# Four bilinear corners weighted and summed in one VectorE instruction each, two biases moved to ScalarE, and a sum of two branches moved to TensorE

## The chip, the cores and the metric

The kernel runs on one core of a Trainium2 chip. The metric is the device time of one execution in microseconds. A core has TensorE (PE, matrix products into PSUM), ScalarE (ACT), VectorE (DVE), GpSimd (POOL, which here issues the indirect gathers) and SyncE (SP, which issues the other transfers). Each engine works through its own list of instructions in order, and the lists meet only in semaphores.

## The reference, cut to what matters

Per image (32 images, 96 channels, 48 x 48 pixels) a first layer ends in `out = (out_mamba + silu(batchnorm(lc))) * gate`, then a 96 x 96 projection, a residual, a layer norm and an MLP whose roundings to half precision and to 8 bits are part of the reference. A second layer is a deformable 3 x 3 convolution: each of the nine taps of a pixel reads the normalised image at a fractional place.

```python
def _bilinear(img, py, px):
    ...
    return (1 - wy_) * (1 - wx_) * v00 + (1 - wy_) * wx_ * v01 + wy_ * (1 - wx_) * v10 + wy_ * wx_ * v11
...
def _qlinear(x, W, b):
    y = q_acc(jnp.einsum('bsk,nk->bsn', q_mul(x), q_mul(W)))
    return q_acc(y + q_mul(b))
```

The samples, times a mask, go through a 9 x 96 x 96 product, again with a residual, a layer norm and an MLP of 384 hidden channels.

## The kernel before

Pass one computes the scan branch and the local branch of all images and stores both. Pass two, which the diff touches, reads them back and does everything else. It walks through **periods** `w` of one chunk of 384 pixels (eight rows): an image has six periods, and a period has twelve **places** `u`. In one period four chunks of work at different stages run side by side: chunk `c` (projection, norm 1, MLP 1), chunk `d` (norm 2's result into the padded image and into a table of corner rows), chunk `e` (deformable convolution, norm 3, MLP 2) and chunk `f` (the last step of MLP 2). Three tiles of 128 pixels are sampled per period, four places for each tile. The order on each engine is written out by hand: every engine's block runs over the same list of `(w, u)` and issues what belongs to a place.

**Sampling.** GpSimd gathers for each tap of a tile one row of 4 corners x 96 channels into `G` (ring of four tiles, nine indirect transfers a tile, issued two tiles ahead). VectorE then treats a tile in two halves (taps 0 to 3, taps 4 to 8). `multiply` (places 0 and 2 of the tile) copies the weights of the half to PSUM, multiplies corner 0 into a PSUM accumulator (L1910) and the corners 1 to 3 in place (L1912). `add_corner` (places 1 and 3) adds them in three instructions (L1925 twice, L1927). TensorE transposes the sums (L1641), ScalarE copies them to `cols_t` (L1791), and at place 3 of a later period `convolve` (L1654) multiplies nine taps into bank BN.

**MLP.** `hidden` (L1678, TensorE) gives three blocks of 128 hidden channels, `rounded` (L1812, ScalarE) rounds them to half precision, `biased` (L1948, VectorE, places 7 and 11) adds the bias and clips at zero, `quantized` (L1819, ScalarE) rounds to 8 bits, `second` (L1686, TensorE) multiplies back. ScalarE rounds the result into `y16` (L1869 or L1832), and `residual` (VectorE, places 9 and 1) adds the second bias (L1955) and the residual (L1957).

**Projection.** At place 0 VectorE writes `xflat` (L1975, the scaled result of norm 2) and adds the local branch to `mix` (L1980). At place 1 TensorE projects `mix` with the gated weights (L1711) and transposes `xflat` (L1721). At place 2 VectorE adds that to `x_t` (L1992) and ScalarE copies the transposed rows to `prow` (L1842). `convolve` waits for `prow`, since bank BN is shared. Behind it TensorE centres `x_t` (L1661), ScalarE squares, TensorE averages (L1668), ScalarE forms the inverse deviation in two steps (L1802, L1805), and VectorE writes `xq` at place 5 (L1940). The chunk `e` does the same with `x3` (L1935, place 5) and ends in another L1940 at place 8. In the last period of an image ScalarE applies SiLU to the whole local branch of the next one (L1881) between two table loads. In two periods of six VectorE computes `positions` (L1550 to L1569) at place 1: those of 12 tiles in one, of 6 in the other.

## Time and profile before

| | us |
|---|---|
| median of three timed runs | 17210.08 |
| lowest and highest | 17208.7, 17227.91 |
| span of the profiled execution (first to last instruction) | 17175.7 |
| median run less that span | 34.4 |
| pass one in that span | 10393 |
| pass two in that span | 6783 |

The profiled execution's own time is shown only as its span; what lies around the span is taken as the 34.4 us by which the median run exceeds it. In the rows below, a timeline row gives the start, the busy time, engine, line, output<-input, the shapes and how many instructions are merged; in square brackets the idle time of the engine before it and what ended the wait. "Places" of the text can be read off by the line numbers.

### The profile page before, as it was taken

The page shows a single profiled execution, that of the slowest core. Times are in us where ns is not written, and L with a number is a line of the kernel's source. Part 1 is how long each engine was busy: PE and PEld are TensorE (multiplying, and loading weights), DVE is VectorE, ACT ScalarE, POOL GpSimd, SP SyncE. Part 2 cuts the span into 40 slices and gives each one's busy share as a digit, 9 for nine tenths or more (in the row PEclk, how much of TensorE's full clock was granted, in tenths as well). Part 3 has the DMA queues.
Part 4 walks back from the last instruction along what each step waited for, and adds up shares of the span by engine and source line. Part 5 has one row for each costly group of instructions (what it writes and reads, how often), then busy time and mean ns, then how long its engine had stood idle before and what let it go on. Part 6 is the DMA issues. An engine that isn't in the chain of part 4 may idle for free. (4 is left out here: it accounts for less than half of the span.)

```text
span 17175.7 us, 183440 instructions
## 1 busy us (share of the span) xinstructions
PE 12732.8 (74%) x51055; PEld 6059.9 (35%) x51055; DVE 14514.2 (85%) x19220; ACT 8968.6 (52%) x16380; POOL 12401.2 (72%) x10756
## 2 busy tenths in 40 slices
PE   6777777777777777777787646777777777777776
PEld 3333333333333333333333312333333333333333
DVE  5888888888888888888888855988898989899998
ACT  4555655656556555565565534444444444444443
POOL 3777777777777777777777744777777777777776
PEclk9999998999999998999999867888888888888887
DMA  2333333333433333333433335666666666666665
GB/s 55 94 97 96 99 100 98 99 95 96 104 94 95 101 98 98 98 98 99 101 97 95 96 90 137 186 187 186 186 188 185 186 192 188 188 188 186 187 188 155
DMA packets 1297936, 2234.90 MB, mean 130 GB/s; under 512 B 713341, under 2 KB 759125, under 8 KB 1284629
## 3 DMA queue, kind: packets, MB, share of 16 engines
q1 hardware_dynamic: 896022, 1090.20, 25.1%
q0 software_dynamic: 368640, 1076.24, 22.3%
q10 hardware_dynamic: 32256, 56.64, 1.1%
q8 instruction: 425, 6.96, 0.2%
q14 instruction: 593, 4.86, 0.1%
HBM read 1493.27 MB, written 275.76 MB: 103 GB/s over the span
## 5 line engine op out<-in xcount | busy, mean ns | idle before, releaser
L1623 POOL DMA_INDIRECT G<-corners,idx x5184 | 4964.2, 958 | 1992.1 <-issue 1554.4
L1383 POOL TENSOR_TENSOR hc<-h,crep 128x768 f32<-128x768 f32 x2304 | 4176.4, 1815 | 2206.5 <-DVE h L1157 1233.9
L1141 DVE TENSOR_TENSOR ps<-dxr,ps 128x768 f32<-128x768 f32 x2304 | 2186.3, 949 | 1041.2 <-PE ps L750 1024.9
L1157 DVE TENSOR_TENSOR_SCAN h<-decay,carry,ps 128x768 f32<-128x768 f32 x1536 | 2776.4, 1808 | 145.5 <-ACT decay L972 85.3
L761 PE MATMUL ps<-hc,sel 128*96 128x512 f32 (+1 forms) x6144 | 2581.8, 548 | 353.4 <-POOL hc L1383 198.7
L972 ACT ACTIVATE decay<-dtr,a_neg 128x768 f32<-128x768 f32 x2304 | 2117.8, 926 | 348.2 <-DVE h L1157 332.8
L750 PE MATMUL ps<-bq,pick 128*128 128x512 bf16 (+1 forms) x4608 | 1233.8, 353 | 991.3 <-DVE h L1157 806.1
L1912 DVE TENSOR_TENSOR G<-G,ps 128x1152 f32<-128x1152 f32 (+1 forms) x1152 | 1724.7, 1497 | 0.0
L761 PEld LDWEIGHTS ps<-hc,sel 128*96 128x96 f32 x6144 | 1022.7, 182 | 1608.1 <-issue 1204.8
L1654 PE MATMUL ps<-cols_t,w_def 128*96 128x384 f32 x3456 | 1342.5, 550 | 178.3 <-ACT prow L1842 172.2
L869 PE MATMUL ps<-xcp,w_local 128*96 128x384 f32 x3456 | 1436.8, 538 | 40.7 <-POOL xcp L1357 39.2
L1925 DVE TENSOR_TENSOR ps<-ps,G 128x384 f32<-128x384 f32 (+1 forms) x2304 | 1407.4, 611 | 47.1
L1157 DVE TENSOR_TENSOR_SCAN h<-decay,ps 128x768 f32<-128x768 f32 x768 | 1342.2, 1748 | 32.3 <-ACT decay L972 2.5
L980 ACT ACTIVATE carry<-h 128x1 f32<-128x1 f32 x1536 | 303.0, 197 | 1934.4 <-DVE h L1157 1932.8
L810 PE MATMUL ps<-xnp,w_conv 128*96 128x384 f32 x3456 | 1292.6, 513 | 24.5 <-ACT x_in L1009 22.3
L1797 ACT ACTIVATE sq<-ps 96x384 f32<-96x384 f32 x576 | 280.1, 486 | 1944.1 <-PE ps L1661 1944.1
L1641 PE MATMUL ps<-ident,G 128*128 128x128 f32 x5184 | 1005.9, 311 | 94.2 <-DVE G L1927 93.1
L750 PEld LDWEIGHTS ps<-bq,pick 128*128 128x128 bf16 x4608 | 377.7, 101 | 1803.2 <-DVE h L1157 923.5
L1791 ACT ACTIVATE cols_t<-ps 128x512 f32<-128x512 f32 (+1 forms) x1728 | 832.8, 483 | 324.2 <-PE ps L1641 323.1
L1641 PEld LDWEIGHTS ps<-ident,G 128*128 128x128 f32 x5184 | 764.0, 162 | 466.6 <-issue 282.9
L1654 PEld LDWEIGHTS ps<-cols_t,w_def 128*96 128x96 f32 x3456 | 626.5, 187 | 831.3 <-issue 598.1
L1686 PE MATMUL ps<-hq,w2q 128*96 128x384 fp8e5 x1152 | 312.0, 389 | 773.8 <-ACT rs L1805 489.4
(243 smaller groups left out, 23803.3 us busy)
## 6 DMA issues: line engine op xcount, KB each, us to landing
crep<-c_rows SPq DMA_DIRECT2D x3072, 96.0 KB
dtr<-rel SPq DMA_DIRECT2D x2304, 96.0 KB, 2.2
dxr<-one_e SPq DMA_DIRECT2D x2304, 96.0 KB
corners<-prow SPq DMA_DIRECT2D x1536, 72.0 KB
G<-corners,idx POOLq DMA_INDIRECT x5184
x_in<-in_x SPq DMA_DIRECT2D x32, 864.0 KB, 6.6
local_all<-local_c ACTq DMA_DIRECT2D x192, 144.0 KB
sim<-sorted_rows SPq DMA_DIRECT2D x32, 864.0 KB, 6.8
```

The source lines that it names most:

```text
L750: m = pe.matmul(wide(bank_of("step", s), P)[:, a:b], Wt["pick"][:, ng, :], M["tall"]["bq"][:, q % 2, a:b], start=True, stop=True)
L761: m = pe.matmul(wide(BY, C)[:, a:b], Wt["sel"][:, cg, :], hc[:, v % HC, a:b], start=(v % ROUND == 0), stop=(v % ROUND == ROUND - 1))
L869: m = pe.matmul(ps[0:C, BV, 0:CH], Wt["w_local"][:, t, :], M["tall"]["xcp"][:, 8 * c + t // 3:8 * c + t // 3 + 8, t % 3:t % 3 + W], start= ...
L972: act.activation(decay[:, s % 3, :], dtr[:, q % 2, cg, :], ACT.Exp, scale=Wt["a_neg"][:, direction(q)[0], ng, cg:cg + 1]).then_inc(S["s_de ...
L1141: dve.tensor_tensor(drive, dxr[:, q % 2, cg, :], drive, ALU.mult).then_inc(S["s_drive"], 1)
L1157: dve.tensor_tensor_scan(along(h[:, v % HR, :], k), along(decay[:, v % 3, :], k), along(wide(bank_of("step", v % STEPS), P), k), first, AL ...
L1383: pool.tensor_tensor(hc[:, v % HC, :], h[:, v % HR, :], crep[:, g % CRING, :], ALU.mult).then_inc(S["s_weighted"], 1)
L1623: pool.indirect_dma_start(M["G"][:, slot(g), k, :], None, table(r), bass.IndirectOffsetOnAxis(M["idx"][side(r)][:, t, k:k + 1], 0)).then_i ...
L1641: m = pe.transpose(ps[:, BT + n % 2, (k % 4) * P:(k % 4 + 1) * P], M["G"][:, slot(t - 1), k, 0:P], ident[:])
L1654: m = pe.matmul(ps[0:C, BN, 0:CH], Wt["w_def"][:, k, :], M["cols"][:, of_e(w)[1] % 2, k, :], start=(k == 0), stop=(k == TAPS - 1))
L1912: dve.tensor_tensor(rows[:, :, 1:], rows[:, :, 1:], by[:, :, 1:].unsqueeze(3).to_broadcast([P, n, CORNERS - 1, C]), ALU.mult).then_inc(S[" ...
L1925: dve.tensor_tensor(acc[:, 0:n], acc[:, 0:n], rows[:, :, q], ALU.add).then_inc(S["p_half"], 1)
```

## The change

VectorE's `multiply` becomes one product over all four corners of the half, in place. `add_corners` sums them with one `tensor_reduce` over the corner axis, that is, it reads four words 96 words apart for each word it writes. The sums of the first half go to a new buffer `samp`, those of the second half over the first half's rows in `G`. The weights are copied to PSUM once in six tiles. ScalarE takes both biases: `biased` in three instructions (one at place 6 or 10, two at 7 or 11), and a second instruction in `returned`. The local branch is no longer added on VectorE: TensorE projects `mix` and `local_t` one after the other into the same bank.

```diff
-                dve.tensor_copy(ps[:, BW, wat:wat + CORNERS * n],
-                                M["wts"][side(r)][:, t, k0:k1].rearrange("p k q -> p (k q)")).then_inc(S["p_wset"], 1)
-                dve.wait_ge(S["p_wset"], at + 1)
-                dve.tensor_tensor(acc[:, 0:n], rows[:, :, 0], by[:, :, 0:1].to_broadcast([P, n, C]),
-                                  ALU.mult).then_inc(S["p_half"], 1)
-                dve.tensor_tensor(rows[:, :, 1:], rows[:, :, 1:],
-                                  by[:, :, 1:].unsqueeze(3).to_broadcast([P, n, CORNERS - 1, C]),
+                if half == 0:
+                    dve.wait_ge(S["p_wset"], n // WGROUP + 1)
+                k0, k1, rows = corners(g, half)
+                by = weights_of(g)[:, k0:k1]
+                dve.tensor_tensor(rows, rows, by.unsqueeze(3).to_broadcast([P, k1 - k0, CORNERS, C]),
                                   ALU.mult).then_inc(S["p_mul"], 1)
...
-                if q < CORNERS - 1:
-                    dve.tensor_tensor(acc[:, 0:n], acc[:, 0:n], rows[:, :, q], ALU.add).then_inc(S["p_half"], 1)
-                else:
-                    dve.tensor_tensor(rows[:, :, 0], acc[:, 0:n], rows[:, :, q], ALU.add).then_inc(S["p_prod"], 1)
+            def add_corners(g, half):
+
+                n = nth(of_tile, g)
+                dve.wait_ge(S["p_mul"], 2 * n + half + 1)
+                if half == 0 and n >= 2:
+                    dve.wait_ge(S["p_tturn"], 3 * (n - 2) + 1)
+                if half == 1:
+                    dve.wait_ge(S["p_prod"], 2 * n + 1)
+                k0, k1, rows = corners(g, half)
+                dve.tensor_reduce(sampled(g, k0, k1), rows.rearrange("p k q c -> p k c q"), AX.X,
+                                  ALU.add).then_inc(S["p_prod"], 1)
...
+            def set_weights(g):
+
+                r, t = of_tile(g)
+                n, size = nth(of_tile, g), CORNERS * TAPS * WGROUP
+                if n >= WGROUP:
+                    dve.wait_ge(S["p_mul"], 2 * (n - WGROUP))
+                at = size * (n // WGROUP % 2)
+                dve.tensor_copy(ps[:, BW, at:at + size],
+                                M["wts"][side(r)][:, t:t + WGROUP].rearrange("p t k q -> p (t k q)")
+                                ).then_inc(S["p_wset"], 1)
...
+            def biased(kind, w, b1, first, last):
+
+                i = turn[kind, w]
+                if first == 0 and turn_before(kind, w):
+                    act.wait_ge(S["p_quant"], NHID * turn_before(kind, w))
+                for j in range(first, last):
+                    act.wait_ge(S["p_rnd"], NHID * i + j + 1)
+                    act.activation(r16[:, KIND[kind], j, :], h16[:, KIND[kind], j, :], ACT.Relu,
+                                   bias=b1[:, j:j + 1]).then_inc(S["p_bias"], 1)
+
+            def returned(n, place, z, b2, done):
+
+                act.wait_ge(S["p_lin" + n], place + 1)
+                act.activation(y16[:, z, :], ps[0:C, BV, 0:CH], ACT.Copy).then_inc(S["p_yr" + n], 1)
+                act.wait_ge(S["p_yr" + n], place + 1)
+                if place:
+                    act.wait_ge(S[done], place)
+                act.activation(z16[:, z, :], y16[:, z, :], ACT.Identity, bias=b2).then_inc(S["p_yb" + n], 1)
...
                 if u == 7 and c is not None:
+                    biased("c", w, Wt["b1q"][0], 1, NHID)
                     quantized("c", w)
...
-                    pe.wait_ge(S["p_mix"], nc_ + 1)
                     if w % NCH == LASTP:
+                        pe.wait_ge(S["p_mamba"], 16 * (next_before(w) + 1))
+                        pe.wait_ge(S["p_silu"], next_before(w) + 1)
                         pe.wait_ge(S["p_gate"], next_before(w) + 1)
...
-                    pe.matmul(ps[0:C, BM, 0:CH], M["tall"]["wg"][:], M["tall"]["mix"][:, part(c[1])], start=True,
-                              stop=True).then_inc(S["p_proj"], 1)
+                    for name in ("mix", "local_t"):
+                        m = pe.matmul(ps[0:C, BM, 0:CH], M["tall"]["wg"][:], M["tall"][name][:, part(c[1])],
+                                      start=(name == "mix"), stop=(name == "local_t"))
+                    m.then_inc(S["p_proj"], 1)
```

The load of the next local branch now waits for the projection instead of the sum.

## Rows read from the trace of the kernel before

**Rows 1.** The page: span and busy time of each engine.

```profile
span 17175.7 us, 183440 instructions
PE 12732.8 (74%) x51055; PEld 6059.9 (35%) x51055; DVE 14514.2 (85%) x19220; ACT 8968.6 (52%) x16380; POOL 12401.2 (72%) x10756
```

**Rows 2.** Windows: pass two, then three periods; stretch: length, PE, PEld, DVE, ACT, POOL, PEclk.

```profile
10393.00:17175.70 6782.70, 4939.76 (x18916) 2443.76 (x18915) 6001.51 (x11201) 3192.66 (x7145) 4964.19 (x5184) 0.80 0.66 184
...
13143.71:13184.79 41.08, 26.69 (x100) 12.38 (x101) 35.21 (x71) 20.75 (x41) 26.58 (x28) 0.79 0.55 150
13184.79:13217.26 32.47, 24.25 (x100) 12.49 (x101) 29.67 (x53) 16.00 (x38) 24.54 (x27) 0.82 0.65 180
13217.26:13253.02 35.76, 25.96 (x100) 12.95 (x101) 33.64 (x71) 15.80 (x38) 27.09 (x29) 0.83 0.63 176
```

**Rows 3.** Timeline of VectorE over one ordinary period.

```profile
13075.42 0.55 DVE L1975 TENSOR_TENSOR xflat<-ps,rs 96x384 f32<-96x384 f32 x1 [0.57 <-ACT rs L1805]
...
13090.71 0.55 DVE L1940 TENSOR_TENSOR xq<-ps,rs 96x384 fp8e5<-96x384 f32 x1 [2.73 <-ACT rs L1805]
...
13098.59 0.55 DVE L1940 TENSOR_TENSOR xq<-ps,rs 96x384 fp8e5<-96x384 f32 x1
13099.06 0.16 DVE L1907 COPY ps<-wts 128x16 f32<-128x16 f32 x1
...
13101.15 0.32 DVE L1955 TENSOR_SCALAR z<-y,b2q 96x384 f16<-96x384 f16 x1
...
13109.56 0.55 DVE L1975 TENSOR_TENSOR xflat<-ps,rs 96x384 f32<-96x384 f32 x1 [0.56 <-ACT rs L1805]
```

**Rows 4.** Timeline of TensorE in the first half of that period.

```profile
13075.38 0.66 PE L1686 MATMUL ps<-hq,w2q 128*96 128x384 fp8e5 x3 [3.63 <-ACT rs L1805]
...
13076.52 1.57 PE L1711 MATMUL ps<-mix,wg 128*96 128x384 f32 x2
...
13079.88 7.52 PE L1654 MATMUL ps<-cols_t,w_def 128*96 128x384 f32 x18 [0.94 <-ACT prow L1842]
```

**Rows 5.** Timeline of ScalarE in its second half.

```profile
13098.03 0.52 ACT L1805 ACTIVATE rs<-rs 96x384 f32<-96x384 f32 x1
13098.46 1.33 ACT L1819 ACTIVATE hq<-r 128x384 fp8e5<-128x384 f16 x3
...
13100.63 0.49 ACT L1869 ACTIVATE y<-ps 96x384 f16<-96x384 f32 x1 [0.36 <-PE ps L1686]
...
13107.06 1.35 ACT L1819 ACTIVATE hq<-r 128x384 fp8e5<-128x384 f16 x3 [2.54 <-DVE r L1948]
```

**Rows 6.** VectorE's groups of the whole span, shapes kept apart: busy, mean ns.

```profile
L1912 DVE TENSOR_TENSOR G<-G,ps 128x1440 f32<-128x1440 f32 x576 | 948.7, 1647 | 0.0
L1912 DVE TENSOR_TENSOR G<-G,ps 128x1152 f32<-128x1152 f32 x576 | 776.0, 1347 | 0.0
...
L1925 DVE TENSOR_TENSOR ps<-ps,G 128x384 f32<-128x384 f32 x1152 | 645.3, 560 | 20.4
...
L1206 DVE TENSOR_REDUCE rlen<-unit 128x19 f32<-128x1824 f32 x32 | 65.2, 2038 | 2.0 <-ACT unit L1026 2.0
...
L1569 DVE TENSOR_TENSOR wts<-up,pos 128x108 f32<-128x108 f32 x64 | 22.8, 357 | 0.0
...
L1566 DVE TENSOR_TENSOR up<-wlow,sig 128x108 f32<-128x108 f32 x32 | 8.7, 272 | 1.1
```

**Rows 7.** Timeline of GpSimd: one of its gathers.

```profile
13102.03 0.95 POOL L1623 DMA_INDIRECT G<-corners,idx  x1 [0.30 <-issue]
```

**Rows 8.** Timeline of VectorE: change of image, then (last row) the small `positions` period.

```profile
13147.23 0.55 DVE L1980 TENSOR_TENSOR mix<-mix,local_t 96x384 f32<-96x384 f32 x1 [2.96 <-ACT local_t L1881]
...
13164.92 0.55 DVE L1940 TENSOR_TENSOR xq<-ps,rs 96x384 fp8e5<-96x384 f32 x1
...
13233.87 0.55 DVE L1940 TENSOR_TENSOR xq<-ps,rs 96x384 fp8e5<-96x384 f32 x1
```

**Rows 9.** Window of one microsecond behind TensorE's pause: PEclk is the granted clock.

```profile
13077.00:13078.00 1.00, 1.00 (x3) 0.33 (x2) 1.00 (x2) 0.77 (x2) 0.70 (x2) 0.50 0.65 191
```

More of the change, by code:

```diff
@@ L380, in build_program @@
                      "p_ctr3", "p_sq3", "p_var3", "p_rs3", "p_xq3", "p_lin3", "p_yr3", "p_yb3", "p_y", "p_out",
-                     "p_wset", "p_mul", "p_half", "p_prod", "p_tturn", "p_cols", "p_conv", "p_x3",
+                     "p_wset", "p_mul", "p_prod", "p_tturn", "p_cols", "p_conv", "p_x3",
                      "p_idx", *[f"p_got{i}" for i in range(GRING)])
@@ L1412 @@
 WTILES = 12
+WGROUP = 6
 def pass_two_memory(sbt, ctx):
@@ L1424, in pass_two_memory @@
     return dict(
-        tall=tall, x2=[low("x2_0", [L]), low("x2_1", [L])], x_t=low("x_t", [L]), local=b("local_t", [C, L]),
+        tall=tall, x2=[low("x2_0", [L]), low("x2_1", [L])], x_t=low("x_t", [L]), local=low("local_t", [L]),
         mix=low("mix", [L]), wg=low("wg", [C]), xn=low("xn2", [PH, PW]), xflat=b("xflat", [C, CH]),
@@ L1435, in pass_two_memory @@
         wts=[b(f"wts{i}", [P, NT, TAPS, CORNERS]) for i in range(2)],
-        G=b("G", [P, GRING, TAPS, CORNERS * C]), cols=b("cols_t", [P, 2, TAPS, CH]), x3=low("x3", [L]))
+        G=b("G", [P, GRING, TAPS, CORNERS * C]), samp=b("samp", [P, 2, SPLIT, P]), cols=b("cols_t", [P, 2, TAPS, CH]), x3=low("x3", [L]))
 def pass_two(nc, ps, S, M, Wt, dram, stages, has, image):
@@ L1522, in landed, with sampled @@
         return sum(slot(w) == slot(g) for w in issued if w <= g)
+    def sampled(g, k0, k1=None):
+        if k0 < SPLIT:
+            ap = M["samp"][:, nth(of_tile, g) % 2]
+        else:
+            k0, k1 = k0 - SPLIT, k1 and k1 - SPLIT
+            ap = M["G"][:, slot(g), 0:SPLIT].rearrange("p k c -> p (k c)")[:, 0:(TAPS - SPLIT) * P].rearrange(
+                "p (k c) -> p k c", c=P)
+        return ap[:, k0] if k1 is None else ap[:, k0:k1, 0:C]
     turns = []
@@ L1896, in multiply @@
             def multiply(g, half):
-                r, t = of_tile(g)
-                at = 2 * nth(of_tile, g) + half
+                n = nth(of_tile, g)
                 if half == 0 and g >= AHEAD:
                     dve.wait_ge(S[f"p_got{slot(g)}"], 16 * TAPS * landed(g))
-                k0, k1, rows, by = corners(g, half)
-                n = k1 - k0
-                if at:
-                    dve.wait_ge(S["p_mul"], at)
-                    dve.wait_ge(S["p_prod"], at)
-                dve.tensor_copy(ps[:, BW, wat:wat + CORNERS * n],
-                                M["wts"][side(r)][:, t, k0:k1].rearrange("p k q -> p (k q)")).then_inc(S["p_wset"], 1)
@@ L1940, in normalize, with residual @@
                 dve.tensor_tensor(dst[:], ps[0:C, bank, 0:CH], rs[:], ALU.mult, **cast).then_inc(S[done], 1)
-            def biased(kind, w, b1):
-                dve.wait_ge(S["p_rnd"], NHID * (turn[kind, w] + 1))
-                if turn_before(kind, w):
-                    dve.wait_ge(S["p_quant"], NHID * turn_before(kind, w))
-                for j in range(NHID):
-                    m = dve.tensor_scalar(r16[:, KIND[kind], j, :], h16[:, KIND[kind], j, :], b1[:, j:j + 1], 0.0,
-                                          ALU.add, ALU.max)
-                m.then_inc(S["p_bias"], 1)
-            def residual(n, c, place, z, b2, res, dst, bsem, done):
-                dve.wait_ge(S["p_yr" + n], place + 1)
-                dve.tensor_scalar(z16[:, z, :], y16[:, z, :], b2, None, ALU.add).then_inc(S[bsem], 1)
-                dve.wait_ge(S[bsem], place + 1)
+            def residual(n, c, place, z, res, dst, done):
+                dve.wait_ge(S["p_yb" + n], place + 1)
                 dve.tensor_tensor(dst[:, part(c)], res[:, part(c)], z16[:, z, :], ALU.add).then_inc(S[done], 1)
@@ L1975, in _ @@
                     dve.tensor_tensor(M["xflat"][:], ps[0:C, BM, 0:CH], M["rs"][:], ALU.mult).then_inc(S["p_xn"], 1)
-                if u == 0 and c is not None:
-                    if p == LASTP:
-                        dve.wait_ge(S["p_silu"], next_before(w) + 1)
-                        dve.wait_ge(S["p_mamba"], 16 * (next_before(w) + 1))
-                    dve.tensor_tensor(M["mix"][:, part(c[1])], M["mix"][:, part(c[1])], M["local"][:, part(c[1])],
-                                      ALU.add).then_inc(S["p_mix"], 1)
                 if p == 1 and u == 1 and has(k):
@@ L1986, in _ @@
                 if u == 1 and f is not None:
-                    residual("3", f[1], nf, 1, Wt["b2q"][1][:], M["x3"], M["x3"], "p_yb3", "p_y")
+                    residual("3", f[1], nf, 1, M["x3"], M["x3"], "p_y")
                 if u == 2 and c is not None:
@@ L1996, in _ @@
                     normalize("1", nc_, BM, M["rs"], M["xq"], "p_xq1", saturate=False)
-                if u == 7 and c is not None:
-                    biased("c", w, Wt["b1q"][0])
                 if u == 8 and e is not None:
@@ L2001, in _ @@
                 if u == 9 and c is not None:
-                    residual("1", c[1], nc_, 0, Wt["b2q"][0][:], M["x_t"], x2[side(c[0])], "p_yb1", "p_x2")
-                if u == 11 and e is not None:
-                    biased("e", w, Wt["b1q"][1])
+                    residual("1", c[1], nc_, 0, M["x_t"], x2[side(c[0])], "p_x2")
                 if of_tile(t) is not None and sub % 2 == 0:
+                    if sub == 0 and of_tile(t)[1] % WGROUP == 0:
+                        set_weights(t)
                     multiply(t, sub // 2)
                 if of_tile(t) is not None and sub % 2 == 1:
-                    for q in range(1, CORNERS):
-                        add_corner(t, sub // 2, q)
+                    add_corners(t, sub // 2)
                 if e is not None and u == 5:
```

40 lines of the change are left out of this document (17 added, 23 removed).

## The prediction, made before the changed kernel ran

> **What bounds the kernel now.** I read the page first for the engines' shares, then the windows by stage, then the timelines of one period. The page shows VectorE busiest with 85% of the span [rows 1]. Only pass two is touched: 6783 us, in which VectorE is busy for 6002, TensorE for 4940, ScalarE for 3193, GpSimd for 4964 [rows 2]. That share is an average. The length of a period varies: 32.5 us in an ordinary one, 35.8 with the small share of `positions`, 41.1 at the change of image [rows 2], and 34.1 for the ordinary period of the timelines [rows 3]; per image the one of each special kind stands beside four ordinary ones.
>
> The timeline shows two halves with different limits. First half, from `xflat` to `xq`: 15.29 us, and VectorE waits 2.73 us at its end [rows 3]. It is a chain through TensorE: `second`, four transposes, projection (started 1.14 us after `second`), transposes of `xflat`, `prow` on ScalarE, then the convolution, 7.52 us for 18 passes, then norm 1 [rows 4]. Second half, from `xq` to the next `xflat`: 18.85 us, in which VectorE waits only 0.56 us [rows 3]. It seems to be bound by VectorE, but two other engines arrive nearly with it: rs of norm 3 ends at 13098.55 [rows 5], and the second L1940 begins at 13098.59 [rows 3]; `y` ends at 13101.12 [rows 5] and `z` begins at 13101.15 [rows 3]. So work taken from VectorE is paid out only as far as these chains allow, and the change lengthens both.
>
> **The products.** 1152 words take 1347 ns and 1440 take 1647 [rows 6], 1.042 ns a word. Extended, 1536 words are 1.75 us and 1920 are 2.15. The product of corner 0, one of its kind a half, and the copy of the weights go. In a queue with no wait an instruction starts some 0.08 us before its forerunner ends: the COPY begins 0.47 us after an xq of 0.55 [rows 3].
>
> **The sums.** Three adds of 384 words (560 ns each [rows 6]) become one reduction that reads 1536 words; for the other half it is 480 and 1920. The trace has a reduction of 1824 adjacent words, 2038 ns [rows 6], so at that rate, with the slope above, 1.74 and 2.14 us: nothing is saved against three adds of 0.56 (1.68). It has none that reads with a hop. What it has is a product that writes every fourth word: 357 ns for 108 words against 272 for the same product written densely, so 0.79 ns more for each word that hops [rows 6]. Applied to the words read, the two reductions are 1.74 + 1536 x 0.79 ns = 2.96 us and 2.14 + 1920 x 0.79 ns = 3.66. The bounds are therefore 1.74 and 2.96, and 2.14 and 3.66. I take the upper ones: a tile's corners lie 96 words apart, no two successive reads adjoin, and the row that is nearest in the pattern is the hopping one, though it hops on the write side.
>
> The Trainium skill (Vector Engine (DVE) Microarchitecture Reference, section 5.2 on measured stream behaviour) says that a port streams at full rate only over runs of at least two adjacent 4-byte words, and gives about 1.73 ns a column for a two-source operation with one source hopping each element. By that figure, as an estimate, the reductions would be 2.8 and 3.5 us and the end some 90 us earlier than by the row. The same section lists a one-source operation alternating between two regions at the full rate, which is the rival below; no run here shows either yet.
>
> **Second half of the period.** VectorE, counted from `xq`, by starts: xq 0.47, first reduction 2.87, x3 at 3.34 (before 2.13), take 0.53, product 2.18, reduction 3.57: the L1940 of norm 3 can go at 9.62. Its own chain hangs on x3 and is 1.21 later than now: 7.88 + 1.20 = 9.08, so VectorE decides. Then 0.47, product 1.67, at 11.76. Here `z` is awaited. ScalarE now puts two bias instructions between rs and hq. Three hq take 1.33 us and one about 0.49, so the spacing is 0.42 to 0.43 [rows 5]: 0.86 for the two. And `z` runs on ScalarE behind `y`, 0.51 instead of VectorE's 0.32 [rows 3]. The residual add, now at 10.79, moves to 10.79 + 1.20 + 0.86 + 0.17 = 13.02, so VectorE waits 1.26 us. Then residual 0.47, reduction 2.87, product 2.18, reduction 3.66: `xflat` at 22.2 against 18.85, +3.4 us. ScalarE's own tail there (three more bias instructions 1.3 us, `z` 0.45, the first two 0.86: 2.6 in all) is paid nearly whole by its present wait of 2.54 us for VectorE's `r` [rows 5]; that chain ends at 18.9 + 1.2 = 20.1 and is hidden as long as the reductions are slow. If they aren't, it bounds the half at 18.9, no better than now.
>
> **First half.** The second projection pair costs what the first does: 1.57 us long, 1.36 from start to start, at a granted clock of 0.50 [rows 4, 9], that is, 1.2 GHz after the pause of 3.63 us [rows 4]. The removed add (0.47 on VectorE) doesn't help: TensorE is in its transposes until 13076.52 in any case. The slow stretch ends during the convolution now: its 18 passes average 0.42 us where the projection's two, with the same columns, average 0.79 [rows 4]. If it still ends at the same time, part of the 1.36 returns, since two passes of the convolution slide out of the slow stretch: 0.7 to 1.4, I take 1.0, so 16.3. VectorE's list, with waits for `z` and the projection met in time, is 0.47 + 1.67 + 0.47 + 2.87 + 0.53 + 2.18 + 3.57 + 1.78 = 13.5 us, hidden.
>
> **Special periods.** `positions` is the busy time by which VectorE exceeds that of an ordinary period: 33.64 - 29.67 = 4.0 us for the small share, 35.21 - 29.67 = 5.5 for the large one [rows 2]; I add 0.2 for the gaps between its short instructions. With the small share the first half takes 16.6 us now (13217.26 to 13233.87 [rows 2, 8]); it becomes 13.5 + 4.2 = 17.7: +1.1. At the change of image VectorE now stands 2.96 us at L1980 for SiLU [rows 8]; that wait moves to TensorE. The half takes 21.2 us now (13143.71 to 13164.92 [rows 2, 8]). Afterwards VectorE needs 13.5 + 5.7 = 19.2, and the chain is SiLU's end at 3.5 us (13147.23 less 13143.71), the projection pair and what follows it in an ordinary period (15.3 - 1.1), with the second pair's 1.4: 19.1. I take 19.3, -1.9. Its second half takes 19.9 now and 22.2 then: +2.3. Transfers: the local branch is requested with `mix`, one projection later, and is wanted a period later, so it is hidden. The wait of the reductions for `p_tturn` is for transposes two tiles back, so nothing queues there. `set_weights` is one short copy in six tiles, 96 in all.
>
> **Sum.** Per image 4 x (1.0 + 3.4) + (1.1 + 3.4) + (-1.9 + 2.3) = 22.5 us; 32 images 720 us. 17176 + 720 = 17896 of span, and with the 34 us around it 17930.
>
> **The rivals.**
> A, the reduction reads at the full rate. For it: 2038 ns for 1824 words, one word a cycle [rows 6]. Against it: those words adjoin. Then the second half is bound by ScalarE at 18.9 (+0.1) and the first by TensorE (+1.0): ordinary +1.1; small share 16.3 - 16.6 + 0.1 = -0.2; change of image -1.9 - 1.0 = -2.9. Sum 1.3 us an image, 42 us: 17250, and with 0.7 to 1.4 for the pair 17210 to 17300.
> B, faster: as A, but the second projection pair costs the chain nothing, because the slow clock ends sooner once TensorE is given that work. Then ordinary periods stay, and what VectorE gains where it binds is kept: 0.0 - 1.2 (small share) - 2.9 - 0.5 (tail of ScalarE shorter than reckoned, 0.1 each period) = -4.6 at best, -147 us, and half of it likelier: 17130. It decides from a full-rate reduction and a pair that adds under 0.3 us an ordinary period. A floor stands below: 27 gathers a period at 0.95 + 0.30 us each [rows 7] are 33.7 us, or 6480 of the 6783 over 192 periods.
> C, hopping costs a whole cycle or more and the longer pauses keep TensorE at the low clock through the convolution: 2.0 ns a word gives 18140, and a further microsecond a period 18300.
>
> **How the numbers follow.** Forecast (reads at 1.6 to 2.0 ns a word) 0.55, its own range 17780 to 18140; A 0.28; B 0.12; C beyond 18140 0.05. The range has to reach A and leaves B's deep end and C out: 17160 to 18140. A measurement tells about 0.2%, 34 us, from no change. Faster by that: B, 0.12, and a little of A, 0.02: 0.14. Within: the lower half of A, 0.14. Slower: the forecast, C and the rest of A, 0.72.
>
> **What would show it.** The two reductions' mean ns (2960 and 3660, or 1740 and 2140) decide first. VectorE's wait before the residual add at place 9, some 1.3 us, on ScalarE's `z`. L1711's successor as four matmuls of about 0.8 us or less in front of the transposes. VectorE's wait before `xq` near 2.8 us (5.5 under A). The wait at L1980 gone and one on TensorE for SiLU in its place. ScalarE's wait for `r` gone. The prediction is wrong if the reductions run at the dense rate, or if the pair is absorbed.

## The result and the profile after

The changed kernel takes 17792.63 us (median of 4 runs, 17774.59 to 17811.11) against 17209.39 for the kernel before: ratio 1.0334, 95% interval 1.0322 to 1.0347, so 583 us slower. The span grew by 597 us, from 17175.7 to 17772.6, all of it in pass two: counted from the first `xflat` (at 10341.5 us before, 10317.3 now) it grew by 621, while what lies ahead of it took 24 less, which is within what it differs by between the traces of these runs (10317 to 10373). The page (busy time of each engine), then the window over pass two:

```profile
span 17772.6 us, 179148 instructions
...
PE 13286.3 (75%) x51439; PEld 6323.8 (36%) x51439; DVE 15213.1 (86%) x12982; ACT 9751.4 (55%) x17916; POOL 12341.4 (69%) x10756
```

```profile
10393.00:17772.60 7379.60, 5485.87 (x19246) 2704.92 (x19246) 6711.85 (x4973) 3959.49 (x8648) 4904.74 (x5184) 0.75 0.60 169
```

VectorE issues 6200 instructions fewer in pass two and is busy 710 us longer (6711.85 less 6001.51 [rows 2]). The groups of the changed kernel between 12000 and 16000 us (count, busy us, mean ns, idle time before) say which:

```profile
L1963 DVE TENSOR_REDUCE G<-G 128x480 f32<-128x1920 f32 x315 | 1097.6, 3484 | 10.8
L1963 DVE TENSOR_REDUCE samp<-G 128x384 f32<-128x1536 f32 x315 | 879.0, 2790 | 0.0
L1951 DVE TENSOR_TENSOR G<-G,ps 128x1920 f32<-128x1920 f32 x315 | 674.2, 2140 | 0.0
...
L1951 DVE TENSOR_TENSOR G<-G,ps 128x1536 f32<-128x1536 f32 x315 | 549.0, 1743 | 5.8 <-DVE ps L1938 0.5
...
L1834 ACT ACTIVATE r<-h,b1q 128x384 f16<-128x384 f16 x630 | 361.1, 605 | 0.0
...
L1844 ACT ACTIVATE z<-y,b2q 96x384 f16<-96x384 f16 x210 | 129.1, 615 | 6.8
L1722 PE MATMUL ps<-local_t,wg 128*96 128x384 f32 x208 | 124.3, 690 | 0.0
...
L1982 DVE TENSOR_TENSOR x<-x_t,z 96x384 f32<-96x384 f32 x105 | 58.9, 561 | 195.7 <-ACT z L1844 195.7
```

The products cost the words at 1.04 ns, as before [rows 6]. The reductions take 2.79 and 3.48 us; the three additions they replace took 1.68 (3 x 0.56 [rows 6]) and 1.98 (3 x 0.66). The last line is VectorE waiting 195.7 us in 105 periods for `z`, now on ScalarE: 1.86 us each, 1.98 in the mean of the ordinary periods. The same period seen in time, on VectorE and then on ScalarE and TensorE:

```profile
13077.73 0.55 DVE L1977 TENSOR_TENSOR xq<-ps,rs 96x384 fp8e5<-96x384 f32 x1 [1.60 <-ACT rs L1817]
13078.20 2.80 DVE L1963 TENSOR_REDUCE samp<-G 128x384 f32<-128x1536 f32 x1
...
13087.06 0.53 DVE L1977 TENSOR_TENSOR xq<-ps,rs 96x384 fp8e5<-96x384 f32 x1
13087.53 1.73 DVE L1951 TENSOR_TENSOR G<-G,ps 128x1536 f32<-128x1536 f32 x1
13091.08 0.55 DVE L1982 TENSOR_TENSOR x<-x_t,z 96x384 f32<-96x384 f32 x1 [1.82 <-ACT z L1844]
...
13099.81 0.56 DVE L2000 TENSOR_TENSOR xflat<-ps,rs 96x384 f32<-96x384 f32 x1
```

```profile
13086.73 1.11 ACT L1834 ACTIVATE r<-h,b1q 128x384 f16<-128x384 f16 x2
13087.74 1.33 ACT L1850 ACTIVATE hq<-r 128x384 fp8e5<-128x384 f16 x3
...
13090.43 0.61 ACT L1844 ACTIVATE z<-y,b2q 96x384 f16<-96x384 f16 x1
```

```profile
13062.03 1.17 PE L1695 MATMUL ps<-hq,w2q 128*96 128x384 fp8e5 x3 [0.87 <-ACT rs L1817]
...
13063.85 1.49 PE L1722 MATMUL ps<-mix,wg 128*96 128x384 f32 x2
13065.13 1.49 PE L1722 MATMUL ps<-local_t,wg 128*96 128x384 f32 x2
...
13068.41 6.02 PE L1663 MATMUL ps<-cols_t,w_def 128*96 128x384 f32 x18 [0.94 <-ACT prow L1872]
```

From `xq` to `xflat` it is 22.08 us here (13077.73 to 13099.81), against 18.85 [rows 3]. In the first half the second projection starts 1.28 us behind the first. The convolution starts 5.90 us after `xflat` (which begins at 13062.51), where it was 4.46, and takes 6.02 us where it took 7.52 [rows 3, 4]: it ends 11.9 us after `xflat` in the one and 12.0 in the other. The granted clock shows why. Two windows of this period, then one of the period before the change [rows 3, 4]; the last number but two is the granted clock, 1.00 is 2.4 GHz and 0.50 is 1.2 GHz.

```profile
13066.00:13067.00 1.00, 1.00 (x5) 0.59 (x4) 1.00 (x1) 0.00 (x0) 0.00 (x0) 0.50 0.00 0
13068.00:13069.00 1.00, 0.59 (x2) 0.41 (x3) 1.00 (x3) 0.15 (x1) 0.69 (x2) 0.99 0.01 1
```

```profile
13082.00:13083.00 1.00, 1.00 (x3) 0.44 (x2) 1.00 (x2) 0.00 (x0) 0.70 (x2) 0.54 0.93 161
```

Now the clock is at its upper level 5.5 us after `xflat`, before the convolution. In the period before the change it came back 7.5 us after `xflat`, inside the convolution.

The period shown before the change was not the usual one. The ordinary periods of a trace are of two kinds: in some the whole convolution runs at the upper level and takes 6.02 us, in the others it starts at the lower one and takes 7.8. Before the change 85 of 123 are of the first kind, with a first half of 13.88 us, and 38 of the second, with 15.87, like the 15.29 of the rows. In the changed kernel 114 of 115 are of the first kind, with 14.62.

The periods of each run can be cut at `xflat` and at the two L1940 (`xq`, and the one for `e`). Means in us over 10450 to 17100 us, by kind of period, worked out from the VectorE timelines; "1st half" is from `xflat` to `xq`, the names are those of the experiments below:

```
                            ordinary (4 an image)       small positions     change of image
                          1st half  2nd half  total     1st   2nd  total    1st   2nd  total
before                      14.50     18.94   33.43   16.52 18.72  35.24  21.17 18.83  40.00
changed                     14.63     22.44   37.08   17.52 21.61  39.13  19.08 22.31  41.39
dense_reads                 15.14     20.11   35.25   15.23 20.17  35.39  19.61 19.00  38.61
two_adds                    17.10     20.08   37.18   15.80 19.43  35.23  19.50 19.43  38.93
two_adds_one_input          15.22     19.15   34.37   15.66 18.82  34.48  19.19 20.35  39.54
mix_on_vector               14.66     22.47   37.13   17.97 21.61  39.58  22.02 22.06  44.08
biases_on_vector            14.33     21.84   36.17   18.01 21.71  39.71  19.38 21.70  41.08
branches_on_tensor          14.91     18.85   33.76   16.27 18.98  35.25  19.04 19.10  38.14
branches_on_tensor_twice    14.96     19.01   33.97   16.44 18.71  35.16  18.40 18.85  37.25
biases_on_scalar            15.10     20.10   35.19   16.16 20.32  36.48  20.83 20.32  41.15
corners_only                15.18     21.86   37.03   18.35 21.69  40.05  22.14 21.68  43.83
```

Changed less before: 4 x 3.65 + 3.89 + 1.39 = 19.9 us an image, 636 us over 32 images, against the 621 from the first `xflat` on (probably because not every chunk is in work in the first and last periods).

### The profile page after: what moved, and what is told of

The parts are those of the page before. It is cut to its first block and busy times, and to the rows that moved or that the text cites. A ratio compares the mean times of both kernels' runs of the same rounds, so it can differ in the third digit from the quotient of the medians.

```text
span 17772.6 us, 179148 instructions
## 1 busy us (share of the span) xinstructions
PE 13286.3 (75%) x51439; PEld 6323.8 (36%) x51439; DVE 15213.1 (86%) x12982; ACT 9751.4 (55%) x17916; POOL 12341.4 (69%) x10756
## 5 line engine op out<-in xcount | busy, mean ns | idle before, releaser
L1633 POOL DMA_INDIRECT G<-corners,idx x5184 | 4904.7, 946 | 2668.5 <-issue 1419.6
L1951 DVE TENSOR_TENSOR G<-G,ps 128x1536 f32<-128x1536 f32 (+1 forms) x1152 | 2236.5, 1941 | 10.3 <-DVE ps L1938 0.5
L1963 DVE TENSOR_REDUCE G<-G 128x480 f32<-128x1920 f32 x576 | 2005.9, 3482 | 19.8
L1963 DVE TENSOR_REDUCE samp<-G 128x384 f32<-128x1536 f32 x576 | 1606.5, 2789 | 0.6
L1663 PE MATMUL ps<-cols_t,w_def 128*96 128x384 f32 x3456 | 1176.4, 496 | 179.0 <-ACT prow L1872 173.1
L1249 DVE TENSOR_SCALAR_CACHE_REDUCE cmp<-sim,dist 128x2304 bf16<-128x2304 f32 (+8 forms) x576 | 844.1, 1467 | 7.8 <-PE ps L857 7.8
L1677 PE MATMUL ps<-sq,mean 128*96 128x384 f32 x1152 | 721.5, 719 | 145.7 <-ACT sq L1809 120.4
L1663 PEld LDWEIGHTS ps<-cols_t,w_def 128*96 128x96 f32 x3456 | 557.3, 166 | 726.2 <-issue 501.1
```

Of the source, the lines that this page charges most:

```text
L1633: pool.indirect_dma_start(M["G"][:, slot(g), k, :], None, table(r), bass.IndirectOffsetOnAxis(M["idx"][side(r)][:, t, k:k + 1], 0)).then_i ...
L1663: m = pe.matmul(ps[0:C, BN, 0:CH], Wt["w_def"][:, k, :], M["cols"][:, of_e(w)[1] % 2, k, :], start=(k == 0), stop=(k == TAPS - 1))
L1951: dve.tensor_tensor(rows, rows, by.unsqueeze(3).to_broadcast([P, k1 - k0, CORNERS, C]), ALU.mult).then_inc(S["p_mul"], 1)
L1963: dve.tensor_reduce(sampled(g, k0, k1), rows.rearrange("p k q c -> p k c q"), AX.X, ALU.add).then_inc(S["p_prod"], 1)
```

## The experiments

The theory after this trace (H): the hop of the reads (they are not adjacent) makes the reduction slow, that is what lengthens the second half, and the work moved elsewhere is nearly hidden behind it. The first rival (M): the moved work is the cost. Times are medians; a ratio is against runs of the kernel before from the same session, whose medians lay between 17209 and 17233 us, so differences between runs of different sessions are good to some 25 us.

**Dense reads.** The same number of words, but adjacent (it sums other words than the corners, so its samples are not the reference's).

```diff
-                dve.tensor_reduce(sampled(g, k0, k1), rows.rearrange("p k q c -> p k c q"), AX.X,
-                                  ALU.add).then_inc(S["p_prod"], 1)
+                near = M["G"][:, slot(g), k0:k1].rearrange("p k (c q) -> p k c q", q=CORNERS)
+                dve.tensor_reduce(sampled(g, k0, k1), near, AX.X, ALU.add).then_inc(S["p_prod"], 1)
```

> The changed kernel with one edit: the reduction reads four adjacent words for each word it writes instead of four words 96 apart; the number of words read and written is the same (it sums other words than the corners, so the samples differ). Theory H (the hop of the reads is the cost): the two reductions fall from 2.79 and 3.48 us to about 1.75 and 2.15, the second half of a period is then set by ScalarE's chain at about 19.3 to 19.8 us, and the time is 17,250 to 17,400. Rival M (the work moved to ScalarE and TensorE is the main cost, and the slow reduction is mostly hidden): the reductions may fall, but the time stays above 17,600. Rival S (a reduction costs 1.8 ns a word here whatever its pattern): 2.79 and 3.48 stay, and so does the time.

17372.6 us, 1.008 of before (1.0063 to 1.0097): some 420 us of the 583 are gone, as H has it. M and S, the rival by which a reduction is slow whatever its pattern, are out. Its groups between 12000 and 16000 us:

```profile
L1964 DVE TENSOR_REDUCE G<-G 128x480 f32<-128x1920 f32 x335 | 721.2, 2153 | 11.4
...
L1964 DVE TENSOR_REDUCE samp<-G 128x384 f32<-128x1536 f32 x335 | 583.0, 1740 | 0.0
L1977 DVE TENSOR_TENSOR xq<-ps,rs 96x384 fp8e5<-96x384 f32 x224 | 123.5, 552 | 421.4 <-ACT rs L1817 421.4
...
L1982 DVE TENSOR_TENSOR x<-x_t,z 96x384 f32<-96x384 f32 x112 | 62.1, 554 | 209.3 <-ACT z L1844 209.3
...
L2000 DVE TENSOR_TENSOR xflat<-ps,rs 96x384 f32<-96x384 f32 x111 | 61.5, 554 | 199.7 <-ACT rs L1817 199.7
```

1.74 and 2.15 us, the dense rate [rows 6]. VectorE now waits for ScalarE in four places (`xq` twice), and the second half takes 20.1 us, a little over the 19.3 to 19.8 expected. The kernel is still 0.8% slower than before. Since a dense reduction takes as long as the three additions, that rest is put down to the moved work, which comes into the open when VectorE is fast; its parts are run by themselves below.

**Two additions** in place of the reduction; the second one waits for the first.

```diff
-                dve.tensor_reduce(sampled(g, k0, k1), rows.rearrange("p k q c -> p k c q"), AX.X,
-                                  ALU.add).then_inc(S["p_prod"], 1)
+                dve.tensor_tensor(rows[:, :, 0:2], rows[:, :, 0:2], rows[:, :, 2:4], ALU.add).then_inc(S["p_half"], 1)
+                dve.wait_ge(S["p_half"], 2 * n + half + 1)
+                dve.tensor_tensor(sampled(g, k0, k1), rows[:, :, 0], rows[:, :, 1], ALU.add).then_inc(S["p_prod"], 1)
```

> The changed kernel with the reduction replaced by two additions: corners 0 and 1 plus corners 2 and 3 in place (768 or 960 words), then the two halves of that into the place where the reduction wrote (384 or 480 words). Theory H: about 0.87 + 0.56 and 1.07 + 0.66 us in place of 2.79 and 3.48; VectorE gives back some 3 us a tile, ScalarE's and TensorE's chains then set the period, and the time is that of the dense reads within 60 us, 17,230 to 17,400. Rival M: above 17,600.

17643.47 us, 1.024 (1.0222 to 1.0257). The additions take 0.95 + 0.56 and 1.16 + 0.66 us, within 0.1 of H's, but the time is 240 us over its range: a miss. M's "above 17,600" was met, and not for M's reason. VectorE stands in a new place (groups, then VectorE's timeline, then GpSimd's):

```profile
L1951 DVE TENSOR_TENSOR G<-G,ps 128x1536 f32<-128x1536 f32 x322 | 563.5, 1750 | 532.4 <-DMA G<-corners,idx 529.6
L1963 DVE TENSOR_TENSOR G<-G 128x960 f32<-128x960 f32 x322 | 373.0, 1159 | 11.0
L1963 DVE TENSOR_TENSOR G<-G 128x768 f32<-128x768 f32 x323 | 305.5, 946 | 0.0
```

```profile
13012.32 0.95 DVE L1963 TENSOR_TENSOR G<-G 128x768 f32<-128x768 f32 x1
...
13023.76 1.75 DVE L1951 TENSOR_TENSOR G<-G,ps 128x1536 f32<-128x1536 f32 x1 [5.42 <-DMA G<-corners,idx]
```

```profile
13012.22 1.88 POOL L1633 DMA_INDIRECT G<-corners,idx  x1 [0.30 <-issue]
13014.40 0.95 POOL L1633 DMA_INDIRECT G<-corners,idx  x1 [0.30 <-issue]
```

A gather that normally takes 0.95 us takes 1.88 when VectorE's addition of 0.95 us, both inputs in SBUF, runs beside it. Of the 2902 gathers that start between 12000 and 16000 us, 646 took over 1 us, up to 2.19, and every one of them had a VectorE instruction with two SBUF inputs beside it; the 1647 that had none took 0.946 in the mean. The mean rises to 1.07 us, 27 x (1.07 + 0.30) = 37 us a period, and that is the length of the ordinary period in the table (37.18). GpSimd sets the pace: it waits for something other than its own issue in only 17.1 of 4000 us. The kernel before keeps one input of each addition in PSUM.

**One input in PSUM.** To tell this from a plain shortage of gathers, the same two additions with their second input from the weights in PSUM (other sums).

```diff
-                dve.tensor_tensor(rows[:, :, 0:2], rows[:, :, 0:2], rows[:, :, 2:4], ALU.add).then_inc(S["p_half"], 1)
+                spread = weights_of(g)[:, k0:k1, 0:1]
+                dve.tensor_tensor(rows[:, :, 0:2].rearrange("p k q c -> p k (q c)"), rows[:, :, 0:2].rearrange("p k q c -> p k (q c)"),
+                                  spread.to_broadcast([P, k1 - k0, 2 * C]), ALU.add).then_inc(S["p_half"], 1)
...
-                dve.tensor_tensor(sampled(g, k0, k1), rows[:, :, 0], rows[:, :, 1], ALU.add).then_inc(S["p_prod"], 1)
+                dve.tensor_tensor(sampled(g, k0, k1), rows[:, :, 0], spread.to_broadcast([P, k1 - k0, C]),
+                                  ALU.add).then_inc(S["p_prod"], 1)
```

> The kernel of the two additions, with the second input of both additions taken from the weights in PSUM (spread over the channels) instead of the other corners in SBUF; same words, same instructions, other sums. Theory P (a VectorE instruction with two SBUF inputs holds up a gather on GpSimd that runs beside it): the gathers' mean falls from 1.07 to about 0.95 us, VectorE's wait for gathers goes, and the time is that of the dense reads or a little below, 17,300 to 17,380. Rival G (a faster VectorE only runs into the gathers' own rate, whatever its inputs): the mean stays 1.07 and the time 17,640.

17261.38 us, 1.003 (1.0018 to 1.0042), a little below the range of theory P, and the gathers are back at their pace (GpSimd's group here, then in the kernel of the two additions):

```profile
L1633 POOL DMA_INDIRECT G<-corners,idx x3063 | 2904.7, 948 | 1095.1 <-issue 869.2 <-PE ps L1651 225.9
```

```profile
L1633 POOL DMA_INDIRECT G<-corners,idx x2903 | 3116.8, 1074 | 884.5 <-issue 867.4 <-PE ps L1651 17.1
```

The additions themselves take as long as before (941 and 1154 ns for the first ones, 946 and 1159 with both inputs in SBUF). So 382 us between the medians, some 360 when each is taken against its own runs of the kernel before, hang on where the second input lies. Rival G is out. The input in PSUM is also one word spread over the channels, and the run does not part the two. The Trainium skill (SBUF — State Buffer, "Who interferes with whom") says that a VectorE instruction with two SBUF inputs contends with GpSimd's reads, and infers that a `tensor_tensor` does not disturb the generation of DMA descriptors. The first agrees with these rows. If the second is taken to cover indirect gathers, it does not hold here.

**The branch sum back on VectorE**, from the changed kernel (the edits of `mix` and the projection undone).

```diff
+                    pe.wait_ge(S["p_mix"], nc_ + 1)
-                    for name in ("mix", "local_t"):
-                        m = pe.matmul(ps[0:C, BM, 0:CH], M["tall"]["wg"][:], M["tall"][name][:, part(c[1])],
-                                      start=(name == "mix"), stop=(name == "local_t"))
-                    m.then_inc(S["p_proj"], 1)
+                    pe.matmul(ps[0:C, BM, 0:CH], M["tall"]["wg"][:], M["tall"]["mix"][:, part(c[1])], start=True,
+                              stop=True).then_inc(S["p_proj"], 1)
...
+                    dve.tensor_tensor(M["mix"][:, part(c[1])], M["mix"][:, part(c[1])], M["local"][:, part(c[1])],
+                                      ALU.add).then_inc(S["p_mix"], 1)
```

> The changed kernel with the sum of the two branches back on VectorE and one projection. Theory H: VectorE waits 0.8 to 2.0 us before xq in ordinary periods, so there the sum is hidden and the shorter projection shortens the first half by at most 1.3 us; the change of image gets its 3 us wait for SiLU back and the small positions period 0.5 us. Per image 4 x (-0.4 +- 0.5) + 0.5 + 2.1: within 60 us of the changed kernel's 17,793. Rival M: the second projection pair costs 1.3 us in each of 192 periods, so 250 us faster.

17907.37 us, 115 above the changed kernel. M is out. H's range is missed by 54 us, mainly in one term: ordinary periods stay (37.13 against 37.08) where -0.4 was expected. The other two are +0.45 and +2.69 (0.5 and 2.1 expected). The ordinary periods show what the pair of matmuls is good for: without it the convolution starts 0.92 us earlier, but only 56 of 113 have it wholly at the upper clock, instead of 114 of 115, and in the mean it takes 0.89 us longer.

**The biases back on VectorE**, from the changed kernel (`biased` and `residual` as before).

```diff
+                if u == 7 and c is not None:
+                    biased("c", w, Wt["b1q"][0])
...
+                if u == 11 and e is not None:
+                    biased("e", w, Wt["b1q"][1])
```

> The changed kernel with both biases back on VectorE. Theory H: VectorE sets the second half of the period, gets 2 x 0.76 us of biases and 0.33 of z there, and loses its wait of 1.8 us for z: about 0 to +0.5 us a period, 17,790 to 17,900. Rival M: ScalarE's longer chain (eight instructions of 0.6 us a period) sets the period, so taking it off makes it over 1 us a period faster, 17,590 or less.

17688.65 us, 104 below the changed kernel and between the two ranges: neither. Cut once more, at the second L1940, the ordinary periods show two effects side by side. From `xq` to there it costs 0.44 us (9.48 to 9.92), where VectorE takes one bias between its reductions. From there to `xflat` it gains 1.04 (12.96 to 11.92): 1.98 us of waiting for `z` go, three quarters of a microsecond of bias and 0.3 of `z` come. So ScalarE's chain costs even beside the slow reduction.

**One part each, from the kernel before.** Biases only:

```diff
-                act.wait_ge(S["p_bias"], turn[kind, w] + 1)
+                    act.wait_ge(S["p_bias"], NHID * turn[kind, w] + j + 1)
...
+                    biased("c", w, Wt["b1q"][0], 1, NHID)
                     quantized("c", w)
```

> The kernel before with one part of the change, both biases on ScalarE. Theory C (the second half of a period is closed by ScalarE's chain as soon as VectorE gives work away): VectorE loses 1.9 us there but ScalarE's eight instructions of 0.6 us lengthen the chain, as they do beside the dense reads, to about 20.1 us against 18.9: +1.2 a period, 17,380 to 17,480. Rival V (VectorE's 85% is what counts): 1.5 us a period faster, 16,900 to 17,000.

17469.83 us, 1.0152 (1.0138 to 1.0166), within the range of theory C; V is out. The second half is 20.10 us as C has it (+1.16). The first is 0.60 longer as well, which C has not: the convolution is wholly at the upper clock in 59 of 120 ordinary periods, instead of 85 of 123. VectorE's waits in it, between 12000 and 16000 us (in total, times, longest):

```profile
DVE xq L1963 <- ACT rs L1805: 280.1, 164, 4.3
DVE x L1968 <- ACT z L1832: 178.3, 110, 1.7
DVE xflat L1986 <- ACT rs L1805: 154.3, 110, 1.4
```

The branch sum only (the edits of `mix`, the projection and the two waits for SiLU and the load, as in the diff of the change):

```diff
+                    for name in ("mix", "local_t"):
+                        m = pe.matmul(ps[0:C, BM, 0:CH], M["tall"]["wg"][:], M["tall"][name][:, part(c[1])],
+                                      start=(name == "mix"), stop=(name == "local_t"))
```

> The kernel before with one part of the change, the sum of the branches by a second projection. If the prediction's terms hold: ordinary periods +0.7 to +1.4, small positions period -0.3, change of image -1.9: +20 to +110 us. If, as the traces of the changed kernel suggest, the slow clock ends sooner and the pair costs 0.1 to 0.6: -90 to +10 us, that is 17,120 to 17,240.

17150.64 us, 0.9964 (0.995 to 0.9978): faster than both kernels, by less than half a per cent, and in the second of the expected ranges. The prediction's +20 to +110 did not come. Ordinary periods pay 0.33 us, the change of image gains 1.86. By the table that is 17 us, and the profiled execution's span is 14 shorter; the timed medians say 60. The sign is clear, its size is not settled. The convolution is wholly at the upper clock in 122 of 123 ordinary periods.

The corners only (product, weights once in six tiles and reduction; biases and sum on VectorE, the two edits above together):

```diff
+                dve.tensor_reduce(sampled(g, k0, k1), rows.rearrange("p k q c -> p k c q"), AX.X,
+                                  ALU.add).then_inc(S["p_prod"], 1)
```

> The kernel before with one part of the change, the product over four corners and the hopping reduction (biases and branch sum stay on VectorE). If parts simply add up (biases +260, branches -60 by their own runs, all together +583): +380, 17,590. If they don't, because VectorE with the slow reduction hides what ScalarE's chain costs alone: the changed kernel less 105 (biases back) plus 115 (branch sum back), 17,750 to 17,850.

17914.54 us, 1.0398 (1.0348 to 1.0449). Both expectations are missed, the sum of the parts by 325 us and the other range by 65. The corners alone cost more than the whole change. The parts add up to 690 + 260 - 60 = 890, the change costs 583. The runs at hand say where the rest goes, each against its own runs of the kernel before: corners 692, corners and biases 674, corners and branch sum 455, all three 583. So beside the corners the biases cost nothing, as long as the branch sum is on VectorE, and the branch sum gains 237 us instead of 60. In the ordinary periods of the corners alone the convolution is wholly at the upper clock in only 31 of 114, and with the branch sum on TensorE in 117 of 117; the first half falls from 15.18 to 14.33 us.

**The second projection in two periods of six**, from the kernel before.

```diff
+    def by_tensor(w):
+        return w % NCH in (1, LASTP)
...
+                    names = ("mix", "local_t") if by_tensor(w) else ("mix",)
+                    for name in names:
```

> The kernel before, with the second projection used only in the two periods of an image in which VectorE sets the first half (the change of image and the one with the small share of positions), and VectorE's sum in the other four. Theory: 1.6 to 2.8 us gained at the change of image, where VectorE no longer waits for SiLU, and 0.5 to 1.0 in the other: 70 to 120 us, 17,110 to 17,160. Rival: TensorE waits for SiLU just as long and its chain gives the gain back: within 30 us of the kernel before.

17159.84 us, 0.9972 (0.9961 to 0.9983): 50 us faster, more than the rival has and less than the 70 to 120 expected. The change of image gains 2.75 us, as much as was thought at best, the small period 0.08 only, and the four ordinary periods, whose instructions were not touched, are 0.54 longer: their convolution is wholly at the upper clock in 64 of 123 instead of 85. No better than the plain form; one would choose that.

**Short hops.** One profiled execution of the changed kernel with each reduction cut into pieces that read with hops of 2, 4 or 8 words (again other sums; only the durations are used).

```diff
+                step = (2, 4, 8)[n % 3]
+                near = M["G"][:, slot(g), k0:k1].rearrange("p k (x q z) -> p k x q z", q=CORNERS, z=step)[:, :, :, :, 0]
+                wide_ = C // step
+                for i in range(step):
+                    m = dve.tensor_reduce(sampled(g, k0, k1)[:, :, wide_ * i:wide_ * (i + 1)], near, AX.X, ALU.add)
```

> The changed kernel with each reduction cut into 2, 4 or 8 (by the tile's number modulo 3) that read with hops of 2, 4 or 8 words inside one corner row; words read and written stay the same in all, the samples differ. Only the durations matter. By the dense rate, a reduction of 768 words (hop 2) takes 0.94 us, one of 384 words (hop 4) 0.54, one of 192 (hop 8) 0.34; by the rate of the hops of 96 words (1.8 ns a word) 1.45, 0.76 and 0.42. Theory L (16 bytes are the unit, two reads in each are enough): hop 2 at the dense rate, hop 4 and 8 slow. Rival Q (pairs of adjacent words are the unit): all three slow. Rival F (only far hops cost): hop 2 and 4 dense.

Groups between 12000 and 16000 us; 768 and 960 words are hop 2, 384 and 480 hop 4, 192 and 240 hop 8:

```profile
L1967 DVE TENSOR_REDUCE G<-G 128x60 f32<-128x240 f32 x818 | 411.1, 573 | 3.5
L1967 DVE TENSOR_REDUCE G<-G 128x120 f32<-128x480 f32 x408 | 386.8, 1010 | 3.5
L1967 DVE TENSOR_REDUCE samp<-G 128x48 f32<-128x192 f32 x824 | 342.9, 484 | 0.0
L1967 DVE TENSOR_REDUCE samp<-G 128x96 f32<-128x384 f32 x408 | 312.7, 826 | 0.0
L1967 DVE TENSOR_REDUCE G<-G 128x240 f32<-128x960 f32 x204 | 225.8, 1148 | 3.5
L1967 DVE TENSOR_REDUCE samp<-G 128x192 f32<-128x768 f32 x204 | 183.5, 938 | 0.0
```

A hop of 2 words (8 bytes) is nearly free: 938 ns for 768 words is what the dense rate gives, and the next 192 words cost 1.09 ns each ((1148 - 938) / 192) against 1.08 in the dense reads ((2153 - 1740) / 384). With a hop of 4 words (16 bytes) a word costs 1.9 ns ((1010 - 826) / 96), with 8 words 1.85 ((573 - 484) / 48), with 96 words 1.81 ((3484 - 2790) / 384). Theory L fits; Q (pairs of adjacent words) and F (only far hops) are out. A hop of 3 words was not run. The Trainium skill (Advanced Engine Details and Errata, "SBUF Cachelines") has it so: at least two accesses have to fall into one 16-byte line; the trace agrees. The rule of adjacent pairs that the prediction takes from the Trainium skill (Vector Engine (DVE) Microarchitecture Reference, section 5.2) would have made a hop of 2 words slow; for this reduction the measurement says otherwise.

## Why the prediction was right, and where it was off

**The number** is right: slower, 17793 us against 17930, inside the range. The range was 980 us wide, and the largest term, the slow reduction, came as forecast. One term did not come as forecast, and it was named beforehand as a sign of being wrong ("if the pair is absorbed").

**The sums**: the step that decided. The upper bound, from a product that writes with a hop, was taken: 2.96 and 3.66 us; measured 2.79 and 3.48. The rate it rests on, 1.83 ns a word, is 1.81 here. Nothing in the rows said that reading with a hop would cost what writing with one does, so that it fits so well is partly luck. Rival A's reading (1.74 and 2.14) is what the dense reads run at, so only the pattern separates the two. The estimate from the 1.73 ns a column of the Trainium skill (Vector Engine (DVE) Microarchitecture Reference, section 5.2), 2.8 and 3.5 us, came nearer than the row, though it is for an operation with two sources.

**The second half**: 22.2 us forecast, 22.44 in the mean of the ordinary periods, 22.08 in the one shown. Two errors met in it. The reductions were sized 0.17 us too long each, so VectorE reaches its wait earlier. And ScalarE's bias instructions were sized too short: they were given the spacing of `hq`, 0.43 us, and take 0.605 and 0.615 us, 0.50 to 0.52 from start to start. So in the period shown `z` was waited for 1.82 us instead of 1.26.

**The first half, ordinary period**: the term that was mis-sized. +1.0 us forecast, +0.13 measured (+0.41 in the branch sum alone). The pair does cost 1.28 us from start to start, and in the mean of the ordinary periods the convolution starts 0.67 us later (5.30 after `xflat` instead of 4.62). But it takes 0.54 us less (6.03 instead of 6.57), because it now runs wholly at the upper clock in 114 of 115 of them and not in 85 of 123. The forecast read the clock from one period, and that was one of the 38 slow ones. Against those the pair saves 1.25 us (15.87 to 14.62); against the 85 it costs 0.74 (13.88 to 14.62).

That moving the branch sum does it is shown by the runs side by side. In the six runs that have it in the ordinary periods the convolution is wholly at the upper clock in 715 of 718 of them, in the five that have not in 295 of 593, with the slow reduction and without it. Three pairs of runs differ in that move alone: 85 of 123 and 122 of 123, 56 of 113 and 114 of 115, 31 of 114 and 117 of 117. The move is the added pair of matmuls and the addition gone from VectorE together; that it is the pair, and how it brings this about, is not shown. TensorE's pause in front of this stretch is no answer: it is 0.85 us in the mean of the changed kernel and 3.1 with the branch sum alone, and the clock rises in time in both. With the slow reduction TensorE spends more of the second half at the lower level, 14.4 us of 22.4 against 5.4 of 18.9; in the period shown that costs VectorE nothing, since from the start of `hq` to the end of `y` it is 2.66 us in both kernels.

**Where the 137 us went** by which 17930 lay too high. The first half of the ordinary periods, four times 0.87 us an image, is 111 us. The second halves and the special periods give back 25 (13 and 12). The sum over 32 whole images, with nothing taken off for pass one, is 39 above the growth of the span. And the 34 us laid around the span are not outside it: in every run whose own span is on record, about 2 us lie outside it. The rest of the 34 is that the profiled execution of the kernel before was shorter than the median; for the changed kernel span and median are 20 apart (17772.6 and 17792.63), which leaves 14.

**The special periods**: first half +1.00 (forecast +1.1) and -2.09 (-1.9). The wait for SiLU did leave VectorE; TensorE now stands 1.60 us before its projection until 13139.76, and SiLU ends at 13139.67. Their second halves are +2.89 and +3.48 (forecast +3.4 and +2.3); the 2.3 was measured against one long example of the kernel before, 19.9, whose mean is 18.83.

**VectorE's wait before `xq`** is 0.8 to 2.0 us instead of 2.8, which is the same error as in the first half. ScalarE's wait for `r` is gone, as forecast.

**Rival A** priced a dense reduction at 17250; it is 17373, since ScalarE's chain gives 20.1 us and not 18.9 for the second half; the bias instructions' 0.6 us are part of that. **Rival B**, faster, needed two things. The pair to be absorbed because the slow clock ends sooner: that came, +0.13 us where B asked for under 0.3. And a dense reduction: that did not. The branch sum alone is the part of B that holds. **Rival C** didn't occur.

## What to carry to other kernels

Fewer instructions is not less time: a reduction over an axis that isn't innermost reads with a hop, and at hops of 16 bytes and more a word took 1.8 to 1.9 ns instead of 1.04 to 1.09; three additions (1.68 us) were faster than one reduction (2.79), and even a dense reduction (1.74) only ties with them. Before moving work from the busiest engine, look who arrives next: here two chains arrived within 0.1 us of it, and work given to ScalarE cost 260 us by itself. An operand's place in PSUM can be what keeps another engine going. And one period of a timeline is one example: before the clock, or a wait, is read from it, count how many periods look like it. Parts of a change run by themselves need not add up, here to 890 us for 583.

## What the runs showed of the hardware that was not expected

- A VectorE addition with both inputs in SBUF (0.95 us) lengthened an indirect gather on GpSimd from 0.95 to 1.88 us; with one input in PSUM the gathers' mean fell from 1074 to 948 ns and the time by some 360 to 380 us.
- A ScalarE instruction with a bias from half precision to half precision took 605 ns for 384 columns; without a bias, to 8 bits, 508. The type written differs too.
- A reduction in SBUF reads at 1.09 ns a word with hops of 2 words, as when dense (1.08), and at 1.8 to 1.9 with hops of 4, 8 or 96.
- With two matmuls added in front of the convolution, and an addition gone from VectorE, the granted clock rose ahead of it: wholly at the upper level in 114 of 115 ordinary periods (85 of 123 before), 6.02 us instead of 7.8 for its 18 passes.
